# Norm sums in a two-layer cross-attention kernel: three chunks added on GpSimd, then one-column matmuls with the products as stationary operand

## Chip, cores, metric

The kernel runs on one core of a Trainium2 chip. The metric is device time in microseconds (us) for one call; lower is better. PE is TensorE, DVE VectorE, ACT ScalarE, POOL GpSimd, SP SyncE. A bank is one of the eight 2 KiB accumulators of PSUM per partition.

## What is computed

Two cross-attention layers one after the other, for 32 batches of 112 queries, 20 heads of 16 channels, 375 context tokens (371 text and 4 image tokens in the second layer). The part that matters here is the second layer's semantic term: the text probabilities of each query and head average the raw context rows, and the length of this average is needed.

```
scores_t = einsum('bhsd,bhtd->bhst', q, k_t) * attn_scale
probs_t = softmax(scores_t, axis=-1)
text_out = einsum('bhst,bhtd->bhsd', probs_t, v_t)
qsem = einsum('bhst,bte->bhse', probs_t, text_ehs)
qsem = _l2norm(qsem)                       # x / max(|x|, 1e-12)
ip_n = _l2norm(ip_ehs)
sem = einsum('bhse,bne->bhsn', qsem, ip_n)
fused = attn_scores + SEM_SCALE * sem      # then a softmax over 4 image tokens
```

## The kernel before

`qsem` is never built. With p the unnormalized probabilities (tokens x queries) and G the Gram matrix of the context rows, |qsem|^2 is the sum over tokens of p * (G p), up to the softmax's denominator. The kernel takes the heads in groups of four (5 groups g = 0 to 4 for a batch, 4 x 112 = 448 columns) and the tokens in three chunks (128, 128, 115 rows). For each group of the second layer:

- `scores`: 12 bf16 matmuls into `ST` (3 banks). ACT takes the exponential twice: into `p32` (stage `scores`, L1133) and, rounded to f32r, into `pr` (stage `p_round`, L1148). There is one `pr`, so ACT's second pass waits until the `y` matmuls of the group before have read it, and the next `scores` wait until it has read `ST`.
- DVE makes `w2` = 2 p32 - pr (L804, 1344 columns, both inputs in SBUF). There are two `w2` buffers, used in turn.
- `y`: 12 f32r matmuls (L715 to L720) give G p in three banks of the ring `R`, one for a chunk; DVE multiplies each into its chunk of `w2` (L801, one input in PSUM, one in SBUF; signal `w_times_y`).
- `pv1`: 12 fp32 matmuls of 21 columns (L732, L736), four of them side by side in strips of 32 columns of the array.
- `ns`: the sum over tokens. Three fp32 matmuls of 448 columns (L745), one for a chunk, each with a 0/1 matrix `sel` of 32 columns as stationary operand, so that group g lands in row g of 32; the three chunks go to partitions 0, 32 and 64 of bank `NS` and add up over the five groups.

After the last group, `ns_copy` (ACT, L1028) copies `NS` to SBUF, `ns_T` transposes it in four pieces (L782, L783), DVE adds the three chunks (L807, `dsum`) and takes the maximum with a bound (L804, `d<-zq,dsum`), ACT takes the root, and the fused softmax follows (`fus`).

An fp32 matmul shows in the trace as two records, each with its own weight load (PEld).

The order of the work is written out by hand in `stage_order()`: a list of stages that every engine walks through in that order, doing its own share of each. Buffers used in turn are noted with `share`: what takes a slot waits for the signal that freed it. `groups1` is the loop over the groups of the second layer; `between` puts other stages in it (loop step 1 ends with `o_mm` of the next batch's first layer, step 2 with its query projection `q`, steps 3 and 4 have nothing behind `ns`). I count loop steps by the g of `groups1`: step g does `scores` of group g, then `y`, `pv1` and `ns` of group g - 1; step 5 has no `scores`. `finish1` is what follows a batch's last group, and `maxima` the stage after that: for the next batch's first layer and this batch's second, score matmuls (L654, L656) go to `ST` (three heads, "wide") and to the pair of banks `PV`, `NS` (two heads, "narrow") in turn, and DVE takes their maxima (L898, L899, L903). Value and Gram matmuls (L629 to L641) run among them. At its end DVE's result is transposed (L663), goes through ACT, GpSimd and a DMA, and lets the next `scores` start (L672).

On GpSimd the kernel before has only subtractions that split numbers into parts, and one product (`vbd`, L1246) for each batch, which waits for a DMA.

Of the kernel before, what the change touches and what calls it, by code (L numbers as in the profile page):

```python
# [49 lines left out]
def stage_order():  # L50
    o = Order()
    later = []
    tile, uses = [0], [0]

# [319 lines left out]
def xattn_two_layers(nc, a, out):  # L374
# [3 lines left out]
    with ctx:  # L378
# [6 lines left out]
        def sem(name):  # L385
# [48 lines left out]
        dsum = sb("dsum", [S, H])  # L434
# [8 lines left out]
        sel = sb("sel_sb", [128, NG, 32])  # L443
        mip = sb("mip_sb", [128, 1])
        bmask = sb("bmask_sb", [H * NIP, C], bf16)
        nss = w2[0][0:96, 0:QW]
# [23 lines left out]
        y_mm, w_times_y, ns_mm, ns_read, ns_T, ns_sum = (  # L470
            sem(n) for n in ("y_mm", "w_times_y", "ns_mm", "ns_read", "ns_T", "ns_sum"))
# [72 lines left out]
        def tensor(e):  # L544
            w = Waiter(e)
            for kind, key in o.stages:
# [54 lines left out]
                elif kind == "weights_done":  # L601
                    w.wait_ge(d_load["small"], 48)
# [136 lines left out]
                elif kind == "ns":  # L739
# [36 lines left out]
                elif kind == "ns_T":  # L776
                    b, = key
                    r = R[slot["R", ("ns_T", b)]]
                    free(w, "R", ("ns_T", b))
                    w.wait_ge(ns_read, b + 1)  # L780
                    for h in range(GH - 1):
                        e.transpose(r[0:S, 96 * h:96 * h + 96], nss[:, S * h:S * h + S], ident[0:96, 0:96])  # L782
                    e.transpose(r[0:S, 288:384], nss[:, 336:448], ident[0:96, 0:96]).then_inc(ns_T, 1)  # L783
# [13 lines left out]
        def vector(e):  # L797
# [11 lines left out]
            for kind, key in o.stages:  # L809
# [47 lines left out]
                elif kind == "weights_done":  # L857
                    w.wait_ge(d_load["small"], 48)
# [54 lines left out]
                elif kind == "p_round":  # L913
# [64 lines left out]
                elif kind == "ns_T":  # L978
                    b, = key
                    by_g = dsum[:].rearrange("p (g h) -> p g h", h=GH)  # L980
# [467 lines left out]
```

## Time and profile before

| | |
|---|---|
| runs shown | 2806.88, 2811.07, 2814.4 us; median 2811.07 |
| profiled execution | 2810.17 us, its span 2808.4 us |
| granted TensorE clock | 0.988 on average |
| PE busy | 2666.7 us, 95% of the span, 25096 matmul records |
| PE weight loads | 2083.7 us, 74% |
| DVE, ACT, POOL busy | 1709.4 (61%), 1253.6 (45%), 468.7 us (17%) |
| chain that ended last | PE 76%, DVE 13%, SPq, ACT and DMA 3% each, issue 2% |

A batch takes about 84.7 us. The page's busy shares are averages over three stages with different limits: the groups of the second layer (about 24 us), the maxima (26 us) and the groups of the first layer (34 us). A matmul record's duration includes its way through the array, so what a record costs is read from the distance between starts.

### The profile page before, as it was taken

Reading aid. Unit: us, or ns where it says so; the run is one execution under the profiler, and the core shown is the slowest. Engines: PE = TensorE matmul, PEld = TensorE weight load, DVE = VectorE, ACT = ScalarE, POOL = GpSimd, SP = SyncE. Lnnn points to the kernel's source line nnn. Section 1 sums busy time; section 2 is a strip of 40 time slices with the busy share of each in tenths; the row PEclk is TensorE's granted clock in tenths of the full one; section 3 lists DMA queues with packets and bytes.
Section 4 is the critical chain, followed back from the end, with each engine's and each line's share of the span. In section 5 each row is a group of like instructions: output and inputs, shape, how many; then the busy total and the mean of one; then the engine's idle time right before and its main releaser. Section 6 shows DMA issues by size and latency. Waiting matters only on the chain.

```text
span 2808.4 us, 61414 instructions
## 1 busy us (share of the span) xinstructions
PE 2666.7 (95%) x25096; PEld 2083.7 (74%) x25096; DVE 1709.4 (61%) x3464; ACT 1253.6 (45%) x2265; POOL 468.7 (17%) x681
## 2 busy tenths in 40 slices
PE   6899999999999999999999999999999999999977
PEld 5677777777777777777777777777777777777755
DVE  3465666765666755666755666655666655667654
ACT  2344444444444444444444444444444444444443
POOL 1111121111121111121111111111111111111100
PEclk8999999999999999999999999999999999999988
DMA  7576546665546765546764556674557665567630
GB/s 196 97 85 87 83 80 83 90 85 84 84 78 84 93 85 81 82 76 90 88 90 79 83 77 86 83 98 76 82 80 88 84 91 80 83 83 85 85 35 7
DMA packets 450078, 236.31 MB, mean 84 GB/s; under 512 B 220459, under 2 KB 449787, under 8 KB 449788
## 3 DMA queue, kind: packets, MB, share of 16 engines
q1 hardware_dynamic: 433958, 209.34, 55.9%
q10 hardware_dynamic: 15840, 23.04, 2.7%
q8 instruction: 199, 3.26, 0.6%
q14 instruction: 81, 0.66, 0.1%
HBM read 166.38 MB, written 64.59 MB: 82 GB/s over the span
## 4 chain that ended last, share of the span: by engine, by line
PE 76%; DVE 13%; SPq 3%; ACT 3%; DMA 3%; issue 2%; POOL 0%; DVEq 0%; ACTq 0%; POOLq 0%
PE R L715 7%; PE ST L672 6%; PE R L569 5%; PE PN L689 5%; PE PN L745 5%; PE R L559 4%; PE R L616 4%; PE PN L732 4%; DVE m L899 4%; PE R L565 3%; PE R L718 3%; PE R L720 3%; PE R L629 3%; PE R L630 3%; PE R L766 2%
## 5 line engine op out<-in xcount | busy, mean ns | idle before, releaser
L1133 ACT ACTIVATE p<-ST 128x1344 f32<-128x1344 f32 x320 | 413.3, 1291 | 155.3 <-PE ST L675 149.5
L715 PE MATMUL R<-pr,Gh 128*128 128x448 f32 (+1 forms) x960 | 369.9, 385 | 28.4 <-DVE acc L801 28.4
L804 DVE SCALAR_TENSOR_TENSOR w<-p,pr 128x1344 f32<-128x1344 f32 x160 | 249.3, 1558 | 227.0 <-ACT pr L1148 227.0
L801 DVE TENSOR_TENSOR rem<-R,kst 128x375 f32<-128x375 f32 (+1 forms) x160 | 87.6, 547 | 485.2 <-ACT kst L1028 485.2
L801 DVE TENSOR_TENSOR w<-R,w 128x448 f32<-128x448 f32 (+1 forms) x480 | 290.7, 622 | 104.0 <-PE R L720 95.5
L629 PE MATMUL R<-wvh,ch 128*128 128x320 f32 (+3 forms) x896 | 302.8, 338 | 11.2 <-DVE cl L801 10.9
L630 PE MATMUL R<-wvh,cl 128*128 128x320 f32 (+3 forms) x896 | 279.6, 312 | 0.0
L672 PEld LDWEIGHTS ST<-Qs,Ks 100*128 100x128 bf16 (+1 forms) x3520 | 189.1, 98 | 88.0 <-issue 32.9
L1194 POOL TENSOR_TENSOR kst<-rem,kst 128x375 bf16<-128x375 f32 (+1 forms) x160 | 146.6, 916 | 618.7 <-ACT kst L1028 319.9
L672 PE MATMUL ST<-Qs,Ks 100*128 100x112 bf16 (+1 forms) x3520 | 228.7, 214 | 15.5 <-DMA Qs<-ms 6.8
L1148 ACT ACTIVATE pr<-ST 128x1344 fp32r<-128x1344 f32 x160 | 205.3, 1283 | 82.2 <-PE R L720 82.2
L715 PEld LDWEIGHTS R<-pr,Gh 128*128 128x128 f32 (+1 forms) x960 | 176.8, 184 | 78.8 <-DVE acc L801 39.7
L632 PE MATMUL R<-wvl,ch 128*128 128x320 f32 (+3 forms) x672 | 210.3, 313 | 0.0
L1194 POOL TENSOR_TENSOR cl<-cT,ch 128x476 fp32r<-128x476 f32 x126 | 157.0, 1246 | 295.6 <-ACT ch L1028 295.6
L1028 ACT ACTIVATE V<-R 128x320 f32<-128x320 f32 (+2 forms) x160 | 70.5, 440 | 288.6 <-PE R L633 288.6
L1028 ACT ACTIVATE kst<-R 128x375 bf16<-128x375 f32 (+1 forms) x160 | 77.6, 485 | 253.8 <-PE R L571 139.1
L1028 ACT ACTIVATE pvt<-PN 128x112 f32<-128x112 f32 (+1 forms) x320 | 97.4, 305 | 187.5 <-PE PN L736 128.9
L903 DVE TENSOR_REDUCE m<-ST 112x3 f32<-112x1113 f32 x128 | 167.9, 1312 | 21.7 <-PE ST L656 18.5
L718 PE MATMUL R<-pr,Gl 128*115 128x448 f32 (+1 forms) x480 | 176.9, 369 | 0.2 <-issue 0.2
L720 PE MATMUL R<-pr,Gl 128*128 128x448 f32 (+1 forms) x480 | 176.3, 367 | 0.0
L629 PEld LDWEIGHTS R<-wvh,ch 128*128 128x128 f32 (+3 forms) x896 | 163.2, 182 | 17.5 <-issue 11.8
L1194 POOL TENSOR_TENSOR qst<-qrem,qst 128x336 bf16<-128x336 f32 x64 | 54.4, 849 | 721.6 <-DVE qst L890 721.6
(178 smaller groups left out, 5761.7 us busy)
## 6 DMA issues: line engine op xcount, KB each, us to landing
Ks<-k_split SPq DMA_DIRECT2D x384, 140.6 KB, 6.4
k_split<-kst SPq DMA_DIRECT2D x128, 281.2 KB, 3.1
Ks<-k_split SPq DMA_DIRECT2D x384, 93.8 KB, 9.4
Qs<-q_split SPq DMA_DIRECT2D x384, 70.0 KB, 9.2
cT<-in_ctxT ACTq DMA_DIRECT2D x30, 750.0 KB, 4.7
q_split<-qst SPq DMA_DIRECT2D x128, 84.0 KB, 2.0
k_split<-kst SPq DMA_DIRECT2D x64, 140.6 KB, 2.9
xT<-in_xT SPq DMA_DIRECT2D x32, 192.0 KB, 3.2
```

Source lines behind the costliest of these rows:

```text
L629: e.matmul(r[0:n, 0:C], h[:, k, 0:n], wh[:, k, :], start=k == 0, stop=False)
L630: e.matmul(r[0:n, 0:C], lo[:, k, 0:n], wh[:, k, :], start=False, stop=False)
L632: e.matmul(r[0:n, 0:C], h[:, k, 0:n], wl[:, k, :], start=False, stop=False)
L672: e.matmul(ST[:, u, S * h:S * h + S], Ks[l][0:m, GH * g + h, 128 * u:128 * u + 128], Qs[l][0:m, GH * g + h, :], start=True, stop=True)
L715: e.matmul(r[0:nj, 0:QW], Gh[0:ROWS[u], q:q + nj], pr[0:ROWS[u], QW * u:QW * u + QW], start=u == 0, stop=False)
L718: e.matmul(r[0:nj, 0:QW], Gl[0:ROWS[u], q:q + nj], pr[0:ROWS[u], QW * u:QW * u + QW], start=False, stop=False)
L720: e.matmul(r[0:nj, 0:QW], Gl[0:nj, GO[j]:GO[j] + nj], pr[0:nj, QW * j:QW * j + QW], start=False, stop=True).then_inc(y_mm, 1)
L801: return e.tensor_tensor(to, x, y, op)
L804: return e.scalar_tensor_tensor(out=to, in0=x, scalar=s, in1=y, op0=op0, op1=op1)
L1028: return e.activation(to, x, ACT.Copy, scale=scale)
L1133: e.activation(p32[i][:].rearrange("p (u q) -> p u q", u=3), st, ACT.Exp).then_inc(p_whole, 1)
L1194: return e.tensor_tensor(to, x, y, ALU.subtract)
```

## The change

GpSimd adds the three chunks of the products in place (two additions of 448 columns for each group, stage `ns_add`). The sum over the remaining 128 partitions is four fp32 matmuls for each group, 20 for a batch: 112 columns of `w2` are the stationary operand, a column of ones moves, and one column of `NS` comes out, queries on partitions as they are needed. The stage `ns` of group g now stands one loop step later, behind `pv1` of group g + 1, and that of the last group in `finish1`. The copy, the transposes, `dsum`, `sel` and its DMA go. Bank `NS` is freed by DVE's maximum (`d_bound`) and no longer by ACT's copy (`ns_read`). The one `R` bank that `ns_T` took in each batch is not taken, so every later user of the ring has another bank than before.

```diff
@@ groups1
-                o.add("ns", b, g - 1, prev)
-                if g == 1:
-                    o.share("NS", 1, ("ns", b), "ns_read", b + 1)
+                o.add("ns_add", b, g - 1, prev)
+            if g > 1:
+                norm_sums(b, g - 2, prev - 1)
             between(g, True)
             prev = n
+
+    def norm_sums(b, g, n):
+        o.add("ns", b, g, n)
+        if g == 0:
+            o.share("NS", 1, ("ns", b), "d_bound", b + 1)
@@ finish1
         turn(b, 1, 1)
-        o.add("ns_copy", b)
         yield
-        o.add("ns_T", b)
-        in_bank(("ns_T", b), "ns_sum", o.at("ns_T", b))
+        norm_sums(b, NG - 1, uses_of[b, 1, NG - 1])
+        o.add("norms", b)
@@ tensor, ns
-                    for j in range(3):
-                        w.wait_ge(w_times_y, 3 * (NG * b + g) + j + 1)
-                        e.matmul(NS[32 * j:32 * j + 32, 0:QW], sel[0:ROWS[j], g, :],
-                                 w2[n % 2][0:ROWS[j], QW * j:QW * j + QW], start=g == 0, stop=g == NG - 1,
-                                 skip_group_check=True).then_inc(ns_mm, 1)
+                    w.wait_ge(ns_added, NG * b + g + 1)
+                    for h in range(GH):
+                        mm = e.matmul(NS[0:S, GH * g + h:GH * g + h + 1], w2[n % 2][:, S * h:S * h + S], one[:], start=True,
+                                      stop=True)
+                    mm.then_inc(ns_mm, 1)
@@ vector, p_round (before w2 is written)
                     if k > 2:
-                        w.wait_ge(ns_mm, 3 * (k - 2))
-                    if k > NG:
-                        w.wait_ge(ns_T, (k - 1) // NG)
+                        w.wait_ge(ns_mm, k - 2)
@@ vector, norms
                     tt(zq[:], zs[:], zs[:], ALU.mult).then_inc(dve_step, own.one())
-                    w.wait_ge(ns_T, b + 1)
-                    parts_sum(by_g, R[slot["R", ("ns_T", b)]][0:S, 0:384].rearrange(
-                        "p (h j g) -> p g h j", j=3, g=32)[:, 0:NG]).then_inc(ns_sum, 1)
-                    w.wait_ge(ns_sum, b + 1)
                     w.wait_ge(dve_step, own.n)
-                    stt(d2[:].rearrange("p (g h) -> p g h", h=GH), zq[:].rearrange("p (g h) -> p g h", h=GH), EPS2 / 2,
-                        by_g, ALU.mult, ALU.max).then_inc(d_bound, 1)
+                    w.wait_ge(ns_mm, NG * (b + 1))
+                    stt(d2[:], zq[:], EPS2 / 2, NS[0:S, 0:H], ALU.mult, ALU.max).then_inc(d_bound, 1)
@@ gpsimd
+                elif kind == "ns_add":
+                    b, g, n = key
+                    k, x = NG * b + g, w2[n % 2]
+                    w.wait_ge(w_times_y, 3 * k + 2)
+                    e.tensor_tensor(x[:, 0:QW], x[:, 0:QW], x[:, QW:2 * QW], ALU.add).then_inc(ns_half, 1)
+                    w.wait_ge(w_times_y, 3 * k + 3)
+                    w.wait_ge(ns_half, k + 1)
+                    e.tensor_tensor(x[0:115, 0:QW], x[0:115, 0:QW], x[0:115, 2 * QW:3 * QW], ALU.add).then_inc(ns_added, 1)
```

PE's program from the last group of a batch (loop step 5) into `maxima`; `pvt` is the transposed output, `sel_sb` the 0/1 matrix. Before:

```order
L720 MATMUL R<-pr,Gl 115x448
L703 MATMUL R<-ident_sb,pvt 112x128 [waits pv_read,w_times_y]
L736 MATMUL PN<-p_0,V 21x112
L745 MATMUL PN<-w_0,sel_sb 32x448
L745 MATMUL PN<-w_0,sel_sb 32x448 [waits w_times_y] x2
L705 MATMUL R<-ident_sb,pvt 112x128 [waits pv_read]
L656 MATMUL ST<-Ks,Qs 112x375
L782 MATMUL R<-ident_sb,w_0 112x96 [waits ns_read]
L783 MATMUL R<-ident_sb,w_0 112x96
L654 MATMUL PN<-Ks,Qs 112x375
L656 MATMUL PN<-Ks,Qs 112x375
L629 MATMUL R<-wvh,ch 128x320 [waits parts_dve,pvT_read]
```

The same place of the changed program:

```order
L724 MATMUL R<-pr,Gl 115x448
L707 MATMUL R<-ident_sb,pvt 112x128 [waits pv_read,w_times_y]
L740 MATMUL PN<-p_0,V 21x112
L749 MATMUL PN<-one,w_1 112x1 [waits ns_added]
L749 MATMUL PN<-one,w_1 112x1 x3
L709 MATMUL R<-ident_sb,pvt 112x128 [waits pv_read,w_times_y]
L660 MATMUL ST<-Ks,Qs 112x375
L749 MATMUL PN<-one,w_0 112x1 [waits ns_added]
L749 MATMUL PN<-one,w_0 112x1 x3
L658 MATMUL PN<-Ks,Qs 112x375 [waits d_bound]
L660 MATMUL PN<-Ks,Qs 112x375
L633 MATMUL R<-wvh,ch 128x320 [waits parts_dve,w_times_y]
```

The sum behind this `pv1` is now that of the group before (`w_1`); the last group's (`w_0`) stands between the wide and the narrow score matmuls, and the narrow ones wait for DVE's maximum.

GpSimd's program over the second-layer groups of one batch, before:

```order
L1194 TENSOR_TENSOR kst<-rem,kst 128x371 [waits k_mid_act]
L1221 COPY kst<-kip 128x3x4 [waits k_low]
L1194 TENSOR_TENSOR qst<-qrem,qst 128x3x112 [waits q_mid,k_ready]
L1246 TENSOR_TENSOR vbd<-vbd,bmask_sb 80x320 [waits d_v]
L1194 TENSOR_TENSOR cl<-cT,ch 128x512 [waits c_hi]
```

And in the changed program, where the two additions of each of the five groups stand around `qst`:

```order
L1205 COPY kst<-kip 128x3x4 [waits k_low]
L1231 TENSOR_TENSOR w_0<-w_0 128x448 [waits w_times_y,k_ready]
L1234 TENSOR_TENSOR w_0<-w_0 115x448 [waits ns_half,w_times_y]
L1231 TENSOR_TENSOR w_1<-w_1 128x448 [waits w_times_y]
L1234 TENSOR_TENSOR w_1<-w_1 115x448 [waits ns_half,w_times_y]
L1177 TENSOR_TENSOR qst<-qrem,qst 128x3x112 [waits q_mid]
L1231 TENSOR_TENSOR w_0<-w_0 128x448 [waits w_times_y]
L1234 TENSOR_TENSOR w_0<-w_0 115x448 [waits ns_half,w_times_y]
L1231 TENSOR_TENSOR w_1<-w_1 128x448 [waits w_times_y]
L1234 TENSOR_TENSOR w_1<-w_1 115x448 [waits ns_half,w_times_y]
L1231 TENSOR_TENSOR w_0<-w_0 128x448 [waits w_times_y]
L1234 TENSOR_TENSOR w_0<-w_0 115x448 [waits ns_half,w_times_y]
```

GpSimd, nearly empty in this stage, now has ten additions there.

## Rows read from the trace of the kernel before

**Rows 1.** Busy us by stage: second-layer groups, maxima (window, length, engines)

```profile
1524.44:1548.88 24.44, 24.44 (x267) 17.99 (x267) 16.04 (x24) 11.14 (x17) 0.83 (x1) 1.00 1.00 100
1548.88:1575.32 26.44, 24.89 (x146) 19.76 (x143) 24.04 (x56) 10.32 (x27) 6.79 (x8) 1.00 0.56 87
```

**Rows 2.** Timeline of PE, loop step 1: start us, duration us, engine, line

```profile
1524.96 0.26 PE L736 MATMUL PN<-p,V 115*21 115x112 f32 x1
...
1525.89 1.33 PE L766 MATMUL R<-wo,x1T 128*112 128x320 f32 x4
```

**Rows 3.** Timeline of PE, loop steps 3 to 5

```profile
1538.36 0.26 PE L736 MATMUL PN<-p,V 115*21 115x112 f32 x1
...
1539.50 0.71 PE L672 MATMUL ST<-Qs,Ks 100*128 100x112 bf16 x11
...
1544.34 0.47 PE L715 MATMUL R<-pr,Gh 128*128 128x448 f32 x1
...
1546.90 0.49 PE L703 MATMUL R<-ident_sb,pvt 128*112 128x128 f32 x3
```

**Rows 4.** Timeline of PE: from narrow strips to full width; one fp32 stream

```profile
1498.39 0.26 PE L692 MATMUL PN<-p,V 119*17 119x112 f32 x1
1498.58 0.71 PE L672 MATMUL ST<-Qs,Ks 102*128 102x112 bf16 x11
...
1532.86 1.39 PE L616 MATMUL R<-x1T,wq 128*128 128x128 f32 x11
```

**Rows 5.** Timeline of ACT and DVE, loop steps 3 and 4

```profile
1537.95 1.29 ACT L1148 ACTIVATE pr<-ST 128x1344 fp32r<-128x1344 f32 x1 [1.22 <-PE R L720]
1542.80 1.29 ACT L1148 ACTIVATE pr<-ST 128x1344 fp32r<-128x1344 f32 x1 [1.20 <-PE R L720]
...
1536.29 1.15 DVE L801 TENSOR_TENSOR w<-R,w 128x448 f32<-128x448 f32 x2
1537.95 0.62 DVE L801 TENSOR_TENSOR w<-R,w 115x448 f32<-115x448 f32 x1 [0.51 <-PE R L720]
1539.27 1.56 DVE L804 SCALAR_TENSOR_TENSOR w<-p,pr 128x1344 f32<-128x1344 f32 x1 [0.70 <-ACT pr L1148]
```

**Rows 6.** Groups by form, POOL: count, busy us, mean ns of one

```profile
L1194 POOL TENSOR_TENSOR cl<-cT,ch 128x512 fp32r<-128x512 f32 x62 | 78.8, 1271 | 92.3 <-ACT ch L1028 92.3
```

**Rows 7.** Timeline of POOL and DVE where both work at once

```profile
1536.52 0.83 POOL L1194 TENSOR_TENSOR qst<-qrem,qst 128x336 bf16<-128x336 f32 x1 [19.49 <-DVE qst L890]
1551.32 0.79 POOL L1246 TENSOR_TENSOR vbd<-vbd,bmask_sb 80x320 f32<-80x320 f32 x1 [13.96 <-DMA vbd<-v_ip]
...
1551.36 0.78 DVE L804 SCALAR_TENSOR_TENSOR d<-zq,dsum 112x20 f32<-112x20 f32 x1
```

**Rows 8.** Timeline, maxima of two batches: transposes ahead, narrow scores, DVE, next `scores`

```profile
1548.88 0.32 PE L705 MATMUL R<-ident_sb,pvt 128*112 128x128 f32 x1
...
1553.12 0.37 PE L654 MATMUL PN<-Ks,Qs 96*112 96x375 bf16 x1 [0.37 <-DVE m L899]
1553.32 0.32 PE L656 MATMUL PN<-Ks,Qs 96*112 96x375 bf16 x1
...
1575.32 0.72 PE L672 MATMUL ST<-Qs,Ks 102*128 102x112 bf16 x11
...
2226.90 0.32 PE L705 MATMUL R<-ident_sb,pvt 128*112 128x128 f32 x1
...
2229.39 0.18 DVE L804 SCALAR_TENSOR_TENSOR d<-zq,dsum 112x20 f32<-112x20 f32 x1
2229.48 0.32 DVE L898 TENSOR_REDUCE m<-PN 112x2 f32<-112x154 f32 x1
...
2252.91 0.22 PE L672 MATMUL ST<-Qs,Ks 102*128 102x112 bf16 x1
```

**Rows 9.** Groups by form, DVE: the two small steps of the norm

```profile
L804 DVE SCALAR_TENSOR_TENSOR d<-zq,dsum 112x20 f32<-112x20 f32 x32 | 8.9, 280 | 1.1
L801 DVE TENSOR_TENSOR zq<-zs 112x20 f32<-112x20 f32 x32 | 8.4, 262 | 0.0
```

More of the change, by code:

```diff
@@ L53, in stage_order @@
     tile, uses = [0], [0]
+    uses_of = {}
     def in_bank(what, signal, value):
@@ L148, in scores @@
         uses[0] += 1
+        uses_of[b, l, g] = n
         o.add("scores", b, l, g, n)
@@ L442, in xattn_two_layers @@
         ident = sb("ident_sb", [128, 128])
-        sel = sb("sel_sb", [128, NG, 32])
+        one = sb("one", [128, 1])
         mip = sb("mip_sb", [128, 1])
         bmask = sb("bmask_sb", [H * NIP, C], bf16)
-        nss = w2[0][0:96, 0:QW]
         wkip = p32[0][:, 0:4 * C].rearrange("p (k c) -> p k c", k=4)
@@ L469, in xattn_two_layers @@
         pv_mm, pv_read, pvT, pvT_read, o_added = (sem(n) for n in ("pv_mm", "pv_read", "pvT", "pvT_read", "o_added"))
-        y_mm, w_times_y, ns_mm, ns_read, ns_T, ns_sum = (
-            sem(n) for n in ("y_mm", "w_times_y", "ns_mm", "ns_read", "ns_T", "ns_sum"))
+        y_mm, w_times_y, ns_half, ns_added, ns_mm = (
+            sem(n) for n in ("y_mm", "w_times_y", "ns_half", "ns_added", "ns_mm"))
         d_bound, d_root, fused, fus_less, ip_exp, ip_weights, ip_T, ip_T_copied, ip_mm, ip_added, num_read = (
@@ L601, in tensor @@
                 elif kind == "weights_done":
-                    w.wait_ge(d_load["small"], 48)
+                    w.wait_ge(d_load["small"], 32)
                 elif kind == "q":
@@ L775, in tensor @@
                     e.transpose(r[0:64, 2 * S:3 * S], x1[b % 2][:, 256:320], ident[0:S, 0:S]).then_inc(x1_T, 1)
[L776 to L783, printed above, removed]
                 elif kind == "ip_T":
@@ L857, in vector @@
                 elif kind == "weights_done":
-                    w.wait_ge(d_load["small"], 48)
+                    w.wait_ge(d_load["small"], 32)
                     w.wait_ge(d_vw, 16)
@@ L977, in vector @@
                         tt(x_[:], r[0:S, 0:C], x_[:], ALU.add).then_inc(x_added, 1)
-                elif kind == "ns_T":
+                elif kind == "norms":
                     b, = key
-                    by_g = dsum[:].rearrange("p (g h) -> p g h", h=GH)
                     w.wait_ge(pvT_read, at("pvT", b, 1, 1))
                     tt(zq[:], zs[:], zs[:], ALU.mult).then_inc(dve_step, own.one())
-                    w.wait_ge(ns_T, b + 1)
-                    parts_sum(by_g, R[slot["R", ("ns_T", b)]][0:S, 0:384].rearrange(
-                        "p (h j g) -> p g h j", j=3, g=32)[:, 0:NG]).then_inc(ns_sum, 1)
-                    w.wait_ge(ns_sum, b + 1)
                     w.wait_ge(dve_step, own.n)
-                    stt(d2[:].rearrange("p (g h) -> p g h", h=GH), zq[:].rearrange("p (g h) -> p g h", h=GH), EPS2 / 2,
-                        by_g, ALU.mult, ALU.max).then_inc(d_bound, 1)
+                    w.wait_ge(ns_mm, NG * (b + 1))
+                    stt(d2[:], zq[:], EPS2 / 2, NS[0:S, 0:H], ALU.mult, ALU.max).then_inc(d_bound, 1)
                 elif kind == "fuse":
@@ L1168, in scalar @@
                     copy(x1T[0:64, 2, 0:S], r[0:64, 2 * S:3 * S]).then_inc(x1_T_copied, 1)
-                elif kind == "ns_copy":
-                    b, = key
-                    w.wait_ge(ns_mm, 3 * NG * (b + 1))
-                    if b:
-                        w.wait_ge(ns_T, b)
-                    copy(nss, NS[0:96, 0:QW]).then_inc(ns_read, 1)
-                elif kind == "ns_T":
+                elif kind == "norms":
                     b, = key
@@ L1204, in gpsimd @@
                     e.memset(g4[:], 0.0)
+                    e.memset(one[:], 1.0)
                     e.memset(x1T[:], 0.0).then_inc(pool_set, 1)
                 elif kind == "weights_done":
-                    w.wait_ge(d_load["small"], 48)
+                    w.wait_ge(d_load["small"], 32)
                 elif kind == "k":
@@ L1290, in sync @@
                         load("wv1")
-                        e.dma_start(sel[:], a["sel"]).then_inc(d_load["small"], 16)
                         e.dma_start(bmask[:], a["bmask"]).then_inc(d_load["small"], 16)
@@ L1414 @@
     kones1[3, TEXT1:KW] = -1e30
-    sel = np.zeros((128, NG, 32), np.float32)
-    for i in range(NG):
-        sel[:, i, i] = 1
     mip = np.ones((128, 1), np.float32)
@@ L1438 @@
         "qone": np.ones((H, S), ml_dtypes.bfloat16),
-        "sel": sel, "mip": mip,
+        "mip": mip,
         "bmask": bmask.reshape(H * NIP, C),
```

5 lines of the change are left out of this document (2 added, 3 removed).

## The prediction

> **What bounds the kernel now.** I read the windows by stage first, since the page's shares average over stages. Among the second layer's groups PE is busy for all 24.44 us, DVE for 16.04, POOL for 0.83; among the maxima PE works 24.89 of 26.44 us and DVE 24.04 [rows 1]. So time taken from PE counts in the first stage; in the second two engines are nearly full, and DVE's lateness counts too. Then the timeline of PE in single loop steps, for what one `ns` costs by the distance between starts, and the timelines of ACT and DVE beside it, for what stands ready behind PE.
>
> In loop step 1 the last `pv1` record starts at 1524.96 and the next full-width matmul at 1525.89, 0.93 later [rows 2]. In step 3, which has nothing behind `ns`, it is 1538.36 to 1539.50, 1.14 [rows 3]; there the third chunk's product ends only at 1537.95 + 0.62 = 1538.57, after `pv1`, and `ns` waits for it [rows 5]. Step 4 is alike, step 5 and step 2 are like step 1. Without any `ns`, going from the narrow strips of a `pv` stage to a full-width matmul takes 1498.58 - 1498.39 = 0.19 [rows 4]. `ns` thus costs 0.74 in three steps and 0.95 in two: 4.1 us a batch.
>
> The limit just behind PE in step 3 is ACT: `pr` ends at 1537.95 + 1.29 = 1539.24, 0.88 after the last `pv1` record, and frees `ST` for the next `scores` [rows 3, 5]. So whatever `ns` saves, a step of this kind cannot give back more than about 0.2 us.
>
> **The change on PE.** Four fp32 matmuls are eight records, each with a weight load of 112 columns and one column moving. No row has a moving operand that small. The nearest is L616: eleven fp32 records with 128-column loads and 128 moving columns in 1.39 us, so about (1.39 - 0.27) / 10 = 0.11 each, the last one's own duration taken as 0.27, near L736's 0.26 [rows 3, 4]. Whichever of the two sides sets this pace, 0.11 is the upper bound if load and matmul go on overlapping. If the load sets it, 112 of 128 columns make 0.098. The lower bound is the bf16 pace of L672, (0.71 - 0.22) / 10 = 0.049, taking 0.22 for its single record [rows 3, 8]. I take 0.098, since these are fp32 loads as L616's are: 8 x 0.098 = 0.78.
>
> The 0.19 for the step to full width, now paid ahead of `ns`, comes on top: the next instruction is reached 0.97 after the last `pv1` record, against 0.93, 1.14, 1.14 and 0.93 in steps 2 to 5. That is +0.04, -0.17, -0.17, +0.04. In step 1 no `ns` stands any more: -0.74 (`o_mm` behind it needs a copy of ACT that is out by then, and DVE's `x_added` for the third chunk's bank just in time). The sum is **-1.00 us** a batch. The fifth `ns` moves into the maxima, in place of the four transposes and their wait for ACT's copy. Its 0.78, and the transposes' gain of some 0.4, I count at nothing: it starts behind the wide scores, and PE stands there for `d_bound` anyway (below). If that cover were gone, the balance would cost 0.4 a batch.
>
> **GpSimd's additions and DVE's port.** An addition has 448 columns, two fp32 inputs in SBUF. The nearest row is `cl`, 512 columns, 1.27 us [rows 6]; a column's share of that makes 1.11, and I take 1.13 for its fixed part. Two are 2.3 us in a step of 1544.34 - 1539.50 = 4.84 us [rows 3], so GpSimd itself keeps up, and PE reads the sums a step later. But `vbd` on POOL ran from 1551.32 to 1552.11, and DVE's small `d<-zq,dsum`, with both inputs in SBUF, took from 1551.36 to 1552.14, 0.78 instead of 0.18: it stood until about 0.15 before POOL's recorded end [rows 7, 8]. DVE's products with an input in PSUM were not held up: two in 1.15 while `qst` ran on POOL from 1536.52 to 1537.35 [rows 5, 7]. The Trainium skill, "SBUF — State Buffer", section "SBUF: two separate sides", says the same of the mechanism: the port pair shared by the two is an exclusive lock for the whole instruction, against a DVE operation with two SBUF inputs. The trace agrees with its 0.78. Without that rule the sum would be 0.51 us a batch lower, by it it stands as follows.
>
> The only two-input DVE work in the stage is L804, 1.56 us, once a step [rows 5]. In step 3 the second product ends at 1536.29 + 1.15 = 1537.44; with some 0.1 to start and 0.07 between, the additions run 1537.54 to 1538.67 and 1538.74 to 1539.87, and L804, ready at 1539.27, starts at 1539.72 and ends at 1541.28. The next two products end at 1542.42, the next additions run 1542.52 to 1543.65 and 1543.72 to 1544.85. `pr` ends at 1542.80 + 1.29 - 0.17 = 1543.92 [rows 5], so L804 is ready at 1543.95, finds the second addition running, starts at 1544.70 and ends at 1546.26. The first product of the last group ends 0.6 later, 1546.86. What waits for it is PE: the `pvT` transposes L703 (1546.90) take that product's bank. L703's load, which carries the wait, starts some 0.2 ahead of its matmul, at 1546.70, and would have been at 1546.36 (less 2 x 0.17); it can go on at about 1546.88. That is a new wait of **+0.51 us** a batch. Behind L703 in PE's queue stand `pv1`, `ns` and all of the maxima. Bounds: nothing, if L804 gets in between the two additions (0.2 us decide it), and 0.9, if it is held for a whole addition.
>
> **The maxima.** The narrow scores now wait for `d_bound`. Before, DVE went from `d` straight to the narrow reduction, 2229.39 to 2229.48, because the scores were long there [rows 8]. Now: `d` 0.18, a signal 0.05, two score matmuls 1553.32 + 0.32 - 1553.12 = 0.52, a signal 0.04 [rows 8], so the reduction starts 0.79 after `d` starts and no longer 0.09: +0.70. One dependent small step less (`dsum`, at most such a step's 0.18 [rows 8]) takes back about 0.14: +0.56 of DVE. `d` has an input in PSUM now and is no longer held up by `vbd`: its mean of 0.28 falls to 0.18, -0.10 (`zq` keeps its 0.26) [rows 9]. Together +0.46.
>
> What that is worth I read from two batches. Where `vbd` cost DVE 0.60, the way from L705 to the next `scores` was 1575.32 - 1548.88 = 26.44; in an undisturbed one 2252.91 - 2226.90 = 26.01 [rows 8]. So 0.43 of 0.60 arrives, and 0.46 x 0.72 = **+0.33 us** a batch. PE itself reaches the narrow scores about 1.4 us later than now; it has 26.44 - 24.89 = 1.55 us of idle time in this stage [rows 1]. Bounds: nothing, and 0.56 in full.
>
> **Sum.** -1.00 + 0.51 + 0.33 = -0.16 us a batch, some 31 times: -5 us. Start and end change by tenths: one DMA less, and an addition more in the last batch's tail. Against the profiled execution's 2810.17 us that is 2805; the median of the runs is 0.9 higher, so **2806 us**. A difference under 0.3% (8.4 us) is what I take as no change.
>
> **The rivals.**
> - L804 slips in between the additions in most batches. For it: 0.2 us is all that separates the two orders, and two latencies of a tenth go into that. Against: the additions would have to be late, and the first block (step 3) is certain. Then -1.00 + 0.33 = -0.67, 31 times: 2790 us.
> - Slower: the lock costs more. If the additions hold L804 for a full 1.13 (they start right at its signal), PE stands 0.85 at L703, and if DVE's 0.56 arrives whole, the batch takes -1.00 + 0.85 + 0.56 = +0.41 more: 2824 us. It decides once wait and lateness together pass 1.0 us. For it: both engines are nearly full among the maxima. Against: the two batches compared above.
> - One-column matmuls don't overlap with their loads. A record would then cost its whole latency, some 0.26 [rows 3], instead of 0.098: 8 x 0.16 = 1.3 us more in four steps, 31 times 5.2: about 2965 us. Against it is L616's 0.11 with a 128-column load each [rows 4]. The Trainium skill, "TensorE: Matmul & The Clock Gate", section "Part 3: Packing small matmuls — row/col tiling", says that a weight load overlaps with running matmuls only where the row group differs; here all loads use the same 128 rows, and by that rule this rival would be the case.
> - The loads are cheaper, at 0.05 a record: step 2 and step 5 give 0.4 each, steps 3 and 4 nothing (ACT), 25 us more: about 2781 us.
> - TensorE's granted clock, 1.00 in these stages [rows 1], falls to its lower level (1.2 GHz) where one column moves; half the first stage at half speed would cost 12 us a batch, some 380 in all. Nothing in [rows 1] speaks for it: both stages run at 1.00 now.
>
> **How the numbers follow.** Chances: the forecast 0.42, slipping in 0.25, slower by the lock 0.22, no overlap 0.05, cheaper loads 0.03, clock 0.03. The range 2786 to 2828 takes in the first three with their bounds and leaves out about 0.15. The forecast alone lies between 2799 and 2815. Faster by over 0.3% (under 2802.6): slipping in, cheaper loads and the lower 0.12 of the forecast, 0.40. Within 0.3%: 0.30 of the forecast and 0.02 of the slower case, 0.32. Slower: 0.28.
>
> **What would show it.** In the changed profile: eight records of the new matmul 0.098 apart and 0.97 from the last `pv1` record to what follows; step 1 shorter by 0.74; additions of 1.1 us; L804's duration well above 1.56 in steps 3 and 4 (it is recorded from its start, the hold-up included); a wait of L703 for DVE's first product of about 0.5; the narrow scores waiting for `d`. The prediction is wrong if L804 keeps 1.56 (faster), if the one-column records stand much over 0.11 apart, or if L705 to the next `scores` grows by more than 0.6.

## The result and the profile after

| | before | after |
|---|---|---|
| median of the runs, us | 2812.74 (2806.88 to 2814.64, 4 runs) | 2863.07 (2860.31 to 2867.24, 4 runs) |
| profiled span, us | 2808.4 | 2860.5 |
| mean granted clock | 0.988 | 0.965 |
| time at the lower clock level, whole span, us | 64.9 | 202.1 |
| the same, stretches that begin between 190 and 2685 us | 0 | 122.9 |

The changed kernel is slower by 1.78% (ratio 1.0178, 95% interval 1.0162 to 1.0193), 50 us, where I had forecast no change. The two last lines of the table are sums over the trace's records of the granted clock.

The page of the changed kernel, busy time first, then groups by form of PE, DVE and POOL:

```profile
PE 2703.1 (94%) x25288; PEld 2208.6 (77%) x25288; DVE 1721.0 (60%) x3432; ACT 1234.7 (43%) x2233; POOL 833.2 (29%) x1002
```

```profile
L749 PE MATMUL PN<-one,w 128*112 128x1 f32 x1280 | 152.1, 240 | 5.0 <-POOL w L1234 1.7
L800 DVE SCALAR_TENSOR_TENSOR w<-p,pr 128x1344 f32<-128x1344 f32 x160 | 282.7, 1767 | 248.8 <-ACT pr L1137 182.0 <-PE PN L749 66.8
L800 DVE SCALAR_TENSOR_TENSOR d<-zq,PN 112x20 f32<-112x20 f32 x32 | 5.6, 175 | 2.0 <-PE PN L749 1.0
L1231 POOL TENSOR_TENSOR w<-w 128x448 f32<-128x448 f32 x160 | 182.8, 1142 | 528.1 <-DVE w L797 528.1
```

PE has 36 us more of busy time, although 20 small matmuls stand where 15 of 448 columns and four transposes stood. `w2` (L804 before, L800 now) goes from 1.56 us [rows 5] to a mean of 1.77, and `d` from 0.28 [rows 9] to 0.175. In 65 of 160 cases (66.8 us of idle time) what `w2` waits for last is not `pr` but PE's `ns`, L749: the sum comes a step later and gives the `w2` buffer back later. For groups 3 and 4 `w2` starts 0.36 us behind the end of `pr` (median), where it was 0.03. My forecast did not have this wait.

The timeline of PE in the changed kernel, from the end of step 4 of one batch to the maxima (a "stand" is time in which PE stands still and waits):

```profile
1489.79 0.54 PE L707 MATMUL R<-ident_sb,pvt 128*112 128x128 f32 x3 [0.60 <-DVE w L797]
...
1490.89 0.26 PE L740 MATMUL PN<-p,V 115*21 115x112 f32 x1
1491.07 0.95 PE L749 MATMUL PN<-one,w 128*112 128x1 f32 x8
1491.88 0.30 PE L709 MATMUL R<-ident_sb,pvt 128*112 128x128 f32 x1
1492.02 0.48 PE L658 MATMUL ST<-Ks,Qs 96*112 96x375 bf16 x2
1492.34 0.32 PE L660 MATMUL ST<-Ks,Qs 96*112 96x375 bf16 x1
1492.81 0.95 PE L749 MATMUL PN<-one,w 128*112 128x1 f32 x8 [0.15 <-POOL w L1234]
1494.44 0.56 PE L658 MATMUL PN<-Ks,Qs 96*112 96x375 bf16 x1 [0.68 <-DVE d L800]
...
1495.91 0.47 PE L633 MATMUL R<-wvh,ch 128*128 128x320 f32 x1
1496.18 0.47 PE L634 MATMUL R<-wvh,cl 128*128 128x320 f32 x1
1496.44 0.47 PE L636 MATMUL R<-wvl,ch 128*128 128x320 f32 x1
...
1497.78 0.35 PE L634 MATMUL R<-wvh,cl 128*128 128x320 f32 x1
```

The two last sums of the batch, L749 for groups 3 and 4, run 1.7 us apart, PE then stands for `d`, and from there the value matmuls of 320 columns (L633 to L636) start 0.27 us apart and last 0.47. At the upper level they start 0.15 apart and last 0.31 (rows of experiment 2). The windows around this place (length, engines' busy time, PEclk is the eighth column) put the fall and the return:

```profile
1456.00:1480.00 24.00, 23.05 (x236) 19.59 (x235) 15.24 (x25) 12.25 (x18) 6.77 (x9) 1.00 0.92 100
1480.00:1494.40 14.40, 13.01 (x150) 10.41 (x148) 10.85 (x21) 5.73 (x7) 7.15 (x7) 1.00 0.95 106
1494.40:1497.80 3.40, 3.36 (x13) 3.26 (x14) 2.28 (x8) 1.50 (x2) 0.45 (x1) 0.51 1.30 123
1497.80:1503.00 5.20, 5.20 (x26) 3.62 (x26) 4.05 (x12) 2.45 (x8) 1.27 (x1) 1.00 0.77 80
```

The granted clock is 1.00 up to the stand, 0.51 (1.2 GHz) for 3.4 us behind it, 1.00 (2.4 GHz) again. Before, the maxima ran at 1.00 [rows 1]. Of the first 30 batches of the changed kernel 28 have one such stretch of 3.4 or 6.8 us in this same place, and between 190 and 2685 us there is none anywhere else. It begins between 0.2 us before and 1.6 us behind the end of the last one-column record, so in some batches before PE stands for `d` at all.

The second and third of PE's longest sums of waits in the changed kernel (total, times, longest); the first, 28.6 us for `acc`, is as before:

```profile
PE PN L658 <- DVE d L800: 24.1, 31, 1.3
PE R L707 <- DVE w L797: 18.6, 32, 0.6
```

To set the clock's part apart from the rest, the table below takes from each trace the mean distance from the first L740 record (L736 before) of one group's `pv1` to that of the next, over batches 3 to 30. The last of these is about 12 us shorter than the others in every kernel and lowers the last two columns by 0.4 to 0.5 us. The first four columns lie in the second layer's loop, the fifth holds its last step, the maxima and the next batch's first layer.

```
kernel         g0-g1  g1-g2  g2-g3  g3-g4  g4-next g0   batch   at lower clock, 190-2685 us
before          6.64   6.80   4.85   4.74   61.18       84.22     0.0
after           5.92   6.86   4.69   5.36   63.05       85.88   122.9
fill            5.92   6.85   4.69   5.37   62.07       84.89    47.8
wide64          5.92   6.83   4.73   5.34   61.76       84.57     3.4
wide34          5.92   6.84   4.69   5.37   61.77       84.59     3.4
wide16          5.92   6.86   4.69   5.37   62.60       85.45    85.3
norms_first     5.92   6.79   4.69   5.37   62.17       84.95    78.5
wide_first      5.93   6.80   4.73   5.34   61.89       84.68     0.0
noadd           5.92   6.83   4.69   4.70   62.87       85.00   105.8
wide_noadd      5.93   6.82   4.73   4.75   61.80       84.03    17.1
bf16            5.92   6.73   4.66   4.56   61.36       83.23    10.2
bf16_c1         5.91   6.69   4.66   4.54   61.41       83.22    17.1
bf16_nolag      6.52   6.89   4.66   4.53   60.82       83.42     6.8
before_c1       6.64   6.75   4.85   6.28   62.69       87.21     0.0
```

The first three columns of the changed kernel came out within 0.02 us of the forecast, the fourth 0.3 over it; together the four are 0.20 us under before. The fifth is 1.87 us longer, and that times 31 is 58 us.

### The profile page after: what moved, and what is told of

Same layout as the page of the kernel before. It is cut to its first block, busy times and chain, and to the rows that moved or that the text cites. A ratio compares the mean times of both kernels' runs of the same rounds, so it can differ in the third digit from the quotient of the medians.

```text
span 2860.5 us, 62247 instructions
## 1 busy us (share of the span) xinstructions
PE 2703.1 (94%) x25288; PEld 2208.6 (77%) x25288; DVE 1721.0 (60%) x3432; ACT 1234.7 (43%) x2233; POOL 833.2 (29%) x1002
## 4 chain that ended last, share of the span: by engine, by line
PE 78%; DVE 9%; SPq 4%; DMA 3%; ACT 3%; issue 3%; POOL 0%; DVEq 0%; ACTq 0%; POOLq 0%
PE ST L676 6%; PE R L719 5%; PE R L573 5%; PE PN L693 5%; PE R L563 4%; DVE w L800 4%; PE R L620 4%; PE R L644 4%; PE PN L749 4%; PE PN L736 4%; PE R L633 3%; PE R L634 3%; PE R L569 3%; PE R L636 3%; PE R L722 3%
## 5 line engine op out<-in xcount | busy, mean ns | idle before, releaser
L800 DVE SCALAR_TENSOR_TENSOR w<-p,pr 128x1344 f32<-128x1344 f32 x160 | 282.7, 1767 | 248.8 <-ACT pr L1137 182.0
L719 PE MATMUL R<-pr,Gh 128*128 128x448 f32 (+1 forms) x960 | 369.0, 384 | 30.0 <-DVE acc L797 28.6
L1231 POOL TENSOR_TENSOR w<-w 128x448 f32<-128x448 f32 x160 | 182.8, 1142 | 528.1 <-DVE w L797 528.1
L633 PE MATMUL R<-wvh,ch 128*128 128x320 f32 (+3 forms) x896 | 320.7, 358 | 10.6 <-DVE cl L797 10.3
L797 DVE TENSOR_TENSOR w<-R,w 128x448 f32<-128x448 f32 (+1 forms) x480 | 283.7, 619 | 56.9 <-PE R L724 48.0
L634 PE MATMUL R<-wvh,cl 128*128 128x320 f32 (+3 forms) x896 | 295.1, 329 | 0.0
L636 PE MATMUL R<-wvl,ch 128*128 128x320 f32 (+3 forms) x672 | 222.3, 331 | 0.0
L633 PEld LDWEIGHTS R<-wvh,ch 128*128 128x128 f32 (+3 forms) x896 | 177.3, 198 | 18.3 <-issue 11.3
L1234 POOL TENSOR_TENSOR w<-w 115x448 f32<-115x448 f32 x160 | 182.6, 1141 | 23.9 <-DVE w L797 1.1
L634 PEld LDWEIGHTS R<-wvh,cl 128*128 128x128 f32 (+3 forms) x896 | 177.6, 198 | 0.3
```

Source lines behind the costliest of these rows:

```text
L633: e.matmul(r[0:n, 0:C], h[:, k, 0:n], wh[:, k, :], start=k == 0, stop=False)
L634: e.matmul(r[0:n, 0:C], lo[:, k, 0:n], wh[:, k, :], start=False, stop=False)
L636: e.matmul(r[0:n, 0:C], h[:, k, 0:n], wl[:, k, :], start=False, stop=False)
L719: e.matmul(r[0:nj, 0:QW], Gh[0:ROWS[u], q:q + nj], pr[0:ROWS[u], QW * u:QW * u + QW], start=u == 0, stop=False)
L797: return e.tensor_tensor(to, x, y, op)
L800: return e.scalar_tensor_tensor(out=to, in0=x, scalar=s, in1=y, op0=op0, op1=op1)
```

## Experiments

Theory A: the clock falls because PE stands for `d_bound`. Theory B: it falls behind the one-column matmuls. Theory C: the loss is not the clock but GpSimd's hold on VectorE. Each edit is against the changed kernel where nothing else is said; each ratio is to the kernel before, run beside it.

**1. `fill`: matmuls in place of the stand.**

```diff
                         free(w, "PV", ("s_max", b, l, h0))
+                        if l == 0 and h0 == 3 and b:
+                            for _ in range(5):
+                                e.matmul(PV[0:S, 0:T], Qs[l][0:96, h0, :], Ks[l][0:96, h0, 0:T], start=True, stop=True)
                         free(w, "NS", ("s_max", b, l, h0))
```

> Five bf16 score matmuls of 320 columns stand ahead of the first narrow score of each batch's last third of maxima, where TensorE otherwise stands about 0.9 us for d_bound; their results are overwritten. THEORY A (the granted clock falls because TensorE stands there): the stretches of 3.4 and 6.8 us at half speed that follow it go, the mean clock comes back from 0.965 to about 0.985, and the run takes about 2863 - 31 x 1.4 = 2820 us. RIVAL B (the stretches of one-column matmuls lower the clock): the stretches stay, 2860 to 2870 us. RIVAL C (GpSimd's additions hold VectorE and that is the cost): clock and time stay too.

2838.85 us, ratio 1.0082 (1.0052 to 1.0111), clock 0.976. Half of the loss went, half stayed. (The added matmuls move 375 columns, as the rows show, not 320.) Thirteen of the first 30 batches still fell; PE's timeline and two windows of one of them:

```profile
1484.88 0.95 PE L752 MATMUL PN<-one,w 128*112 128x1 f32 x8 [0.15 <-POOL w L1237]
1485.69 1.65 PE L658 MATMUL PN<-Ks,Qs 96*112 96x375 bf16 x5
1487.13 0.52 PE L661 MATMUL PN<-Ks,Qs 96*112 96x375 bf16 x1
```

```profile
1480.00:1487.13 7.13, 6.38 (x60) 4.71 (x59) 5.50 (x16) 2.17 (x4) 3.06 (x3) 0.91 1.17 118
1487.13:1490.50 3.37, 3.37 (x17) 3.22 (x16) 2.33 (x8) 0.88 (x1) 0.00 (x0) 0.68 1.35 141
```

There is no stand at all between the last one-column matmul and the scores, and the clock falls all the same, at 1485.8 by its records. So the stand adds to it but is not needed: A by itself is not enough.

**2. `wide64`: the same loads, 64 columns moving.**

```diff
-        one = sb("one", [128, 1])
+        one = sb("one", [128, 64])
-                        mm = e.matmul(NS[0:S, GH * g + h:GH * g + h + 1], w2[n % 2][:, S * h:S * h + S], one[:], ...
+                        mm = e.matmul(NS[0:S, GH * g + h:GH * g + h + 64], w2[n % 2][:, S * h:S * h + S], one[:], ...
```

> The ones are 64 columns wide and each matmul of the norm's sum writes 64 equal columns, of which the next one leaves one standing, so that TensorE moves 64 columns for each weight load and not one. THEORY B (one-column matmuls lower the clock): the stretches at half speed go, mean clock about 0.985, 2820 us. THEORY A (the stand for d_bound lowers it): they stay, 2860 to 2870 us, as long as a record still stands 0.10 us behind the last; if it is 0.13, 2866 to 2885 us.

2824.55 us, 1.0033 (1.0019 to 1.0047), clock 0.986: 38 of the 50 us are back by moving 63 columns that nobody reads. The stand is untouched, first in the waits, then in one batch with its windows:

```profile
PE PN L658 <- DVE d L800: 22.0, 31, 1.2
```

```profile
1470.95 1.00 PE L749 MATMUL PN<-one,w 128*112 128x64 f32 x8
1472.59 0.37 PE L658 MATMUL PN<-Ks,Qs 96*112 96x375 bf16 x1 [0.64 <-DVE d L800]
...
1473.10 0.31 PE L634 MATMUL R<-wvh,cl 128*128 128x320 f32 x1
1473.25 0.30 PE L636 MATMUL R<-wvl,ch 128*128 128x320 f32 x1
1473.39 0.31 PE L633 MATMUL R<-wvh,ch 128*128 128x320 f32 x1
```

```profile
1466.00:1472.59 6.59, 5.26 (x55) 3.88 (x53) 5.58 (x16) 1.57 (x3) 2.26 (x2) 1.00 1.16 113
1472.59:1476.00 3.41, 3.41 (x21) 3.11 (x22) 2.67 (x10) 1.73 (x4) 0.80 (x1) 1.00 1.27 139
```

The eight records take 1.00 us where they took 0.95, and their starts stand 0.098 apart in both, so it is not the moved columns that set the pace; by what the forecast worked out, it is the weight loads. The same stand of 0.64 us follows, and the clock stays at 1.00. One stretch at the lower level is left in the middle of the run, where there were 36 times 3.4 us. Theory B had named 2820 us.

**3. `wide34`: 64 columns for groups 3 and 4 only.**

```diff
+                    m = 64 if g > 2 else 1
                     for h in range(GH):
-                        mm = e.matmul(NS[0:S, GH * g + h:GH * g + h + 1], w2[n % 2][:, S * h:S * h + S], one[:], ...
+                        mm = e.matmul(NS[0:S, GH * g + h:GH * g + h + m], w2[n % 2][:, S * h:S * h + S], one[:, 0:m], ...
```

> 64 columns of ones in the sums of groups 3 and 4 alone, which run within some 4 us of each other and just ahead of the stand for d_bound; one column in groups 0 to 2. THEORY B' (it is the one-column stretches next to the stand that the clock falls after): nearly all of what 64 columns everywhere gave, 2825 to 2830 us, clock 0.985. If each of the five stretches adds its share wherever it stands: 2840 to 2850 us.

2825.39 us, 1.0034 (1.0021 to 1.0046), clock 0.985. It is the two stretches next to each other and to the stand that matter; whether one of them would do was not tried. The three one-column stretches amid dense matmuls cost the clock nothing.

**4. `wide16`: as 2, with 16 columns.**

> 16 columns of ones in place of 64 or 1, all else as in the changed kernel. THEORY B in its weak form (the clock answers to the columns that TensorE moves): between the two, at 2835 to 2855 us, with some of the stretches at half speed left. If what matters is only that the matmul is not one column wide: as with 64, 2825 us.

2850.46 us, 1.0120 (1.0099 to 1.0141), clock 0.970, 85.3 us at the lower level. So it is not "one column or more": 16 give back a third of what 64 do (12.6 of 38.5 us; by the ratios, two fifths).

**5. `norms_first`, and 6. `wide_first` with 64 columns as well: VectorE's `norms` ahead of the wide maxima.**

```diff
         turn(b, 1, 1)
+        o.add("norms", b)
         yield
         norm_sums(b, NG - 1, uses_of[b, 1, NG - 1])
-        o.add("norms", b)
         yield
```

> VectorE makes zq and d ahead of the wide maxima of the same step and not behind them; TensorE's order is the same. TensorE's stand for d_bound goes down from about 0.9 to 0.45 us. THEORY A: fewer stretches at half speed, about half of the 1.4 us a batch back, 2835 to 2850 us. RIVAL B: clock as it is, and only the 0.3 to 0.4 us of the shorter stand, 2850 to 2860 us.

2836.35 us, 1.0079 (1.0050 to 1.0108), clock 0.971. The wait for `d` falls from 24.1 to 10.5 us and a third of the time at the lower level goes with it.

> Both edits at once: 64 columns of ones, and zq and d ahead of the wide maxima. THEORY B (the one-column matmuls are what the clock falls after, the stand for d_bound only adds to it): no stretch at half speed in the middle of the run, the shorter stand is worth 0.4 us a batch beside the 64-column kernel, 2824.5 - 12 = 2812 us, as before within 0.2%. If the order of VectorE's work is worth nothing once the clock stays up, 2824 us.

2828.23 us, 1.0040 (1.0027 to 1.0052), clock 0.987. My 12 us did not come: with the clock up the order is worth nothing. The waits of PE say where the gain went; of `wide_first`:

```profile
PE PN L658 <- DVE m L895: 17.9, 34, 0.6
...
PE PN L658 <- DVE d L800: 10.4, 31, 0.3
```

```profile
PE R L784 <- DVE fus L797: 11.9, 31, 3.8
```

`d` gives 11.6 us, the maxima behind it take 5.4 of them, and `fus`, at 3.8 us with 64 columns alone, takes 8.1. VectorE has the same work in the stage, and PE waits for it in another place. With the clock up, then, a shorter stand is worth nothing; it helps where one-column matmuls stand ahead of it and the clock falls. The 26.7 us of `norms_first` are more than its 44 us less at the lower level would bring by the rate of experiment 2 (38.5 us for 119.5, 0.32 each: 14 us). PE's waits for `d`, for the narrow scores' maxima and for `fus` together are 7.0 us less than in the changed kernel; where the rest is from is not settled.

**7. `before_c1`: the kernel before with one-column matmuls added.**

```diff
                         w.wait_ge(w_times_y, 3 * (NG * b + g) + j + 1)
+                        if g > 2 and j == 2:
+                            for h in range(GH):
+                                e.matmul(NS[0:S, QW + h:QW + h + 1], w2[n % 2][:, S * h:S * h + S], mip[:], start=True,
+                                         stop=True, skip_group_check=True)
                         e.matmul(NS[32 * j:32 * j + 32, 0:QW], sel[0:ROWS[j], g, :],
```

> The kernel before, with four one-column matmuls (8 records) more in the norm's part of groups 3 and 4, into columns that nobody reads; nothing else of the change, so no late sum and hardly a stand for d_bound. They add 2 x 0.79 us a batch, 49 us in all: 2863 us. THEORY B (one-column stretches here are enough by themselves): stretches at half speed as in the changed kernel, 40 us more, 2895 to 2905 us, clock 0.965. THEORY AB (it takes them and the stand together): no or few stretches, 2855 to 2868 us, clock 0.985.

2905.04 us, 1.0326 (1.0303 to 1.0349), clock 0.988: no stretch at the lower level in the middle of the run, so one-column matmuls in groups 3 and 4 are not enough where `sel`'s dense matmuls stand on both sides of them and nothing stands for `d`; which of the two spares the clock this run does not tell. (Their start flag falls in the bank in which the norm's sums grow; the norms are changed by it.) The time lies at the upper end of what I had written for theory B, but by luck: the clock did not fall. It is 42 us over what I had expected without the clock. The timeline of PE shows why:

```profile
1506.05 0.92 PE L750 MATMUL PN<-w,sel_sb 128*32 128x448 f32 x4
1506.90 0.95 PE L748 MATMUL PN<-mip_sb,w 128*112 128x1 f32 x8
1507.77 0.94 PE L750 MATMUL PN<-w,sel_sb 115*32 115x448 f32 x2
1508.64 0.47 PE L716 MATMUL R<-pr,Gh 128*128 128x448 f32 x1
```

The two records of the third chunk take 0.87 us by themselves and the four of the others 0.85; in the kernel before, whose row follows, all six take 1539.50 - 1538.44 = 1.06 to the scores of [rows 3]:

```profile
1538.44 1.13 PE L745 MATMUL PN<-w,sel_sb 128*32 128x448 f32 x6
```

The three chunks go to three strips of 32 columns and run side by side; my matmuls cut them apart. That is 0.66 us, twice a batch, 31 times: 41 us, the surplus.

**8. `noadd`, and 9. `wide_noadd` with 64 columns: no additions on GpSimd.** The stage `ns_add` does nothing and `ns` waits for `w_times_y` of all three chunks.

> GpSimd adds nothing; the sum over partitions takes the first of the three token chunks alone, so this leaves chunks 2 and 3 out of the norm. RIVAL C (the additions' hold on VectorE is the main cost): L800 comes back from 1.77 to 1.56 us, the wait of L707 goes, and most of the 50 us with them, 2815 us. THEORY A: the hold alone is worth 0.5 us a batch and goes, the wait for d_bound stays at 0.9 us, the clock stays at about 0.965, 2840 to 2850 us.

2834.33 us, 1.0070 (1.0048 to 1.0092), clock 0.967, between the two expectations. Time came back, 29 us, but the clock did not. DVE's group in `noadd` and the waits:

```profile
L800 DVE SCALAR_TENSOR_TENSOR w<-p,pr 128x1344 f32<-128x1344 f32 x160 | 249.4, 1559 | 249.0 <-ACT pr L1137 181.9
```

```profile
PE PN L658 <- DVE d L800: 35.6, 31, 1.7
```

`w2` is back at 1559 ns, the wait of L707 is gone, PE comes earlier and stands longer for `d`, and the clock falls in all of the first 30 batches. C names a cost that is there, and not a small one, but my forecast had it in its sum; with the additions gone, the fall of the clock is still there. The two costs stand side by side: 38.5 us come back with the clock (2), 29 here, and 57 with both (9).

> 64 columns of ones and no additions on GpSimd (chunks 2 and 3 are left out of the norm). The clock stays at 0.985, so that the difference to the 64-column kernel is the price of the additions alone. From the prediction's own term (0.5 us of wait in L707 in each batch) 2824.5 - 16 = 2809 us. If the additions also cost through L800 in the other steps (1.77 against 1.56 us, five times a batch), 2824.5 - 32 = 2792 us.

2806.15 us, 0.9957 (0.9942 to 0.9973), clock 0.984. Beside `wide64`, the ratios differ by 0.0076, 21 us or 0.69 us a batch, give or take 6 us by their intervals; the batch of the table gives 0.54. That is the additions' price. It does not contradict the 0.51 of my term, and it is below the 32 us of the other expectation. L800 is longer for groups 1, 3 and 4, but only the last of these, ahead of L707, has PE waiting.

The clock did not stay up throughout. In 5 of the first 30 batches it fell, 17.1 us in all, with no one-column matmul in the kernel. PE's stand for `d` is longer here than in `wide64`:

```profile
PE PN L658 <- DVE d L800: 34.2, 31, 1.6
```

So the clock can fall behind 64 moving columns too where the stand is long (1.1 us on average, against 0.7 and one such batch in `wide64`), only far less often than behind one: `noadd`, with nearly the same stand, has 30 such batches.

**10. `bf16`: products in bf16, three chunks summed in PSUM, no additions, `norms` early.**

```diff
+                        wb = w2[n % 2][0:nj, QW * j:QW * j + QW // 2].bitcast(bf16)
-                        tt(wj, R[slot["R", ("y", n, j)]][0:nj, 0:QW], wj, ALU.mult).then_inc(w_times_y, 1)
+                        tt(wb, R[slot["R", ("y", n, j)]][0:nj, 0:QW], wj, ALU.mult).then_inc(w_times_y, 1)
...
+                        for j in range(3):
+                            wj = w2[n % 2][0:ROWS[j], QW * j:QW * j + QW // 2].bitcast(bf16)
+                            mm = e.matmul(NS[0:S, GH * g + h:GH * g + h + 64], wj[:, S * h:S * h + S], one[0:ROWS[j], :],
+                                          start=j == 0, stop=j == 2)
```

> VectorE writes its three products of a step as bf16, GpSimd adds nothing, and 12 matmuls of 64 columns a step with bf16 weights sum partitions and chunks in PSUM (all three chunks are in the norm); zq and d ahead of the wide maxima. If a bf16 load of 112 columns stands 0.05 us behind the last, a stretch takes 0.6 us and not 0.79: 2812 - 16 (no hold) - 5 = 2791 us. If it stands 0.10 us, 1.2 us: 2812 - 16 + 5 x 0.4 x 31 = 2858 us less what lies in TensorE's waits, about 2840 us.

2779.25 us, 0.9864 (0.9848 to 0.9879), clock 0.985: 1.4% faster than the kernel before, and 12 us better than my lower number; which of the three edits brings the surplus was not tried. The products are rounded to bf16 here. PE's group of the new sum and one stretch of it:

```profile
L751 PE MATMUL PN<-one,w 128*112 128x64 bf16 x1280 | 119.8, 218 | 0.0
L751 PE MATMUL PN<-one,w 115*112 115x64 bf16 x640 | 109.6, 217 | 0.0
```

```profile
1529.11 0.81 PE L751 MATMUL PN<-one,w 128*112 128x64 bf16 x12
1529.85 0.47 PE L719 MATMUL R<-pr,Gh 128*128 128x448 f32 x1
```

Twelve records to the next instruction in 1529.85 - 1529.11 = 0.74, the records 0.052 apart in the trace, against 0.81 for the eight of fp32 (1491.07 to 1491.88, above).

**11. `bf16_c1`: as 10, with one column of ones.**

> The bf16 kernel (2779 us) with one column of ones in place of 64. THEORY B: its 12 one-column matmuls a step are again followed by stretches at half speed, 20 to 40 us more, 2800 to 2820 us. If the shorter stretches (0.6 us for 0.8) are short enough: 2779 us.

2778.12 us, 0.9873 (0.9853 to 0.9892), clock 0.982. No different from 64 columns; 17.1 us at the lower level remain. I had expected 20 to 40 us more. The short stand for `d` (10.5 us in all) is not enough to explain it: `norms_first` has the same 10.5 us and 78.5 us at the lower level. What sets the two apart is the sum itself (twelve bf16 records for eight fp32) and the additions with PE's waits for them, 18.9 us at L707 in `norms_first`; which of these spares the clock the run does not say.

**12. `bf16_nolag`: as 10, each group's sum in the step of its own products.** `norm_sums(b, g - 1, prev)` stands right behind `pv1` of group g - 1, and none in `finish1`.

> The bf16 kernel with each group's sum in the step of its own products, as in the kernel before, and not a step later. d no longer waits for a late sum: the 0.34 us a batch that TensorE stands for d_bound go, 2779 - 10 = 2769 us. If the sum then stands for the third product instead, five times a batch, 2779 us or more.

2788.56 us, 0.9904 (0.9888 to 0.9921). Slower than with the lag, and the stand for `d` did not go: it is 14.3 us in all, against 10.5. Step 1 gets its 0.60 us back on the bill (6.52 against 5.92 in the table), and the fifth column gives only 0.54 for it; the rest is in the second column.

## Why the prediction was wrong

The step that failed is the last rival, the clock, and what lay under it: every term of the sum was priced at the granted clock of before. I had given the fall 0.03 and dismissed it because "both stages run at 1.00 now". That a stretch runs at 1.00 in the kernel before says nothing about a kernel that takes the dense matmuls out of just that stretch. The size I gave it (half the first stage, 380 us) was no help either: the fall came elsewhere, among the maxima, for 3.4 us a batch. Measured: moving 64 columns in place of one brings 1.31 us a batch back (85.88 to 84.57), 41 us of the span and more than the 35 us by which the result lay above my range. The runs with fewer such stretches lie in between, as table and ratios show. The Trainium skill, "TensorE: Matmul & The Clock Gate", section "A second HAM failure mode: psum-queue depth-cycling", tells of a clock that drops where the engine is idle briefly but often between groups of matmuls. The stand's part agrees with it: with the stand filled 13 batches fall and not 28 (1), and with 64 columns one falls behind stands of 0.7 us (2) and five behind stands of 1.1 (9). That the clock falls behind matmuls that move one column, with a stand or without, and behind the same ones moving 64 in one batch of 30, is shown by experiments 1 and 2 alone.

The cause is thus shown in two halves. Of the changed kernel's fall the one-column fp32 matmuls of groups 3 and 4 are the main part (2, 3). The surrounding is the other: with the stand taken out 13 batches still fall (1), with a long stand and 64 columns 5 fall (9), and in the kernel before, with dense matmuls around the one-column ones and no stand for `d`, none does (7). Why a given batch falls and another does not stays open.

Point by point, the other terms, at the upper clock (`wide64` against before, where 0.35 us a batch remain to be explained and I had forecast -0.16):
- Step 1, -0.74: measured 6.64 to 5.92, -0.72. Right.
- Steps 2 and 3, +0.04 and -0.17: 6.80 to 6.83 and 4.85 to 4.73 (4.69 with one column), +0.03 and -0.12 (-0.16). Right; records 0.098 apart, as the loads had it, and 0.99 from the last `pv1` record to the next instruction, for 0.97. The rule of the Trainium skill ("TensorE: Matmul & The Clock Gate", section "Part 3: Packing small matmuls — row/col tiling") by which a load on the same rows does not overlap with running matmuls went with the 2965 us; the trace is against what I had worked out from it, with records of 0.24 us standing 0.098 apart.
- Step 4, -0.17 and +0.51 for the lock: +0.60. Without additions it is 4.70 (one column) and 4.75 (64), so the saving is 0.04 at most and not 0.17, and the lock 0.6. Part of the missing saving went to the late sum, which I had not priced: with no additions L707 still starts 0.27 us behind the last `y` matmul, and 0.31 with 64 columns, where it was 0.20 before (medians), because `w2` of group 4 waits for `ns` of group 2. The mechanism of the lock is as foretold (rows below). L800 at 1486.75 lasts 2.25 us and ends at 1489.00; less its 1.56 it was let go at 1487.44, 0.15 before the addition's recorded end at 1487.59, as `vbd` let `d` go in [rows 7]. L707 then waits 0.60.

```profile
1486.44 1.15 POOL L1234 TENSOR_TENSOR w<-w 115x448 f32<-115x448 f32 x1
1486.75 2.25 DVE L800 SCALAR_TENSOR_TENSOR w<-p,pr 128x1344 f32<-128x1344 f32 x1 [1.03 <-PE PN L749]
```

- Last step and maxima, +0.04 and +0.33: 61.18 to 61.76, +0.58. Too small by 0.2. I priced the wait for `d_bound` alone; `ns` of group 4 also waits for the last addition (0.15 at 1492.81), and `d` stands behind both. The gain at `fus` I did not see at all, its wait fell from 19.7 us to 3.8 in a run.

The sizes wrong at the upper clock make 0.5 us a batch, 16 us; they alone would have left the result within my range. The clock's 41 us did not.

## What to carry to other kernels

When a change replaces dense matmuls by small ones, the granted clock is a term of its own: look for the places where the small matmuls come to stand beside waits of TensorE, not for the stage with the most of them, and give the fall a price from a stretch at each level. Where weight loads set the pace anyway, a wider moving operand is nearly free (0.03 us for eight records here) and is the cheapest test and cure. Before putting work on GpSimd, see which two-input operation of VectorE follows its trigger: here five times 2.3 us of an "idle" engine cost 0.5 to 0.7 us on the path each batch. The three kernels that let PSUM do the adding of bf16 products ran 1.0 to 1.4% faster than the kernel before, at the price of rounding the products. And ask which buffer a sum that comes a step later keeps occupied.

## What the runs showed of the hardware

- 64 fp32 columns cost next to nothing beside one in these matmuls: the eight records start 0.098 us apart in both, last 1.00 us against 0.95, and the instruction behind them comes 0.03 us later.
- Behind 1, 16 and 64 moving columns, with the same loads and about the same stand, 28, 21 and 1 of the first 30 batches had a stretch at the lower clock level.
- bf16 products as stationary operand stand 0.052 us apart (112 columns loaded), fp32 ones 0.098 for each of two records: twelve matmuls over three chunks in bf16 (0.74 us) take less of PE than four over one in fp32 (0.81).
- Three fp32 matmuls on separate strips of 32 columns ran in 1.06 us together and in 0.85 and 0.87 us when cut into two and one.
- Matmuls with the start flag in other columns of a bank changed sums that were growing in that bank (7; the output moved by 0.31 of its size).
